# One attention block with a mixture of experts on one core: h and hn stored in two parts on other queues, the last ranks and slots earlier, and tile 2 in two passes

## The reference, cut to what matters

```python
def _layernorm(x, axis=-1, eps=1e-05):
    m = jnp.mean(x, axis=axis, keepdims=True)
    v = jnp.var(x, axis=axis, keepdims=True)
    return (x - m) / jnp.sqrt(v + eps)
...
    def _L0_xattn_ref(query, key):
        a = jnp.einsum('bqd,bkd->bqk', query, key)
        e = jax.nn.softmax(a, axis=-1)
        c = jnp.einsum('bqk,bkd->bqd', e, key)
        return c

    def _L0_ffn_ref(x, W_gate, b_gate, W_e, b_e):
        TOP_K = 2
        logits = x @ W_gate + b_gate
        _, top_idx = jax.lax.top_k(logits, TOP_K)
        y_all = jax.nn.relu(jnp.einsum('bsd,edh->bseh', x, W_e) + b_e)
        y = jnp.take_along_axis(y_all, top_idx[..., None], axis=2)
        return y.mean(axis=2)
    x = x + jnp.tanh(g_xattn[0]) * _L0_xattn_ref(_layernorm(x, axis=-1), ctx_4096)
    x = x + jnp.tanh(g_ffn[0]) * _L0_ffn_ref(_layernorm(x, axis=-1), L0_ffn_W_gate, L0_ffn_b_gate, L0_ffn_W_e, L0_ffn_b_e)
    return x
```

## Time and profile before

| | us |
|---|---|
| median of 3 runs | 343.68 (340.76 to 344.42) |
| the profiled execution | 344.42 |
| its span, first to last instruction | 342.5 |
| TensorE busy in the span | 319.5 (93%) |
| VectorE, ScalarE, GpSimd busy | 203.9, 122.9, 75.3 |
| mean granted TensorE clock | 0.98 |

### The profile page before, as it was taken

How to read it: one execution, slowest core, us unless ns; L and a number is a source line. 1 busy time by engine, 2 the same in 40 slices (tenths; PEclk the granted TensorE clock), 3 DMA queues, 4 the chain that set the end, 5 groups by cost and what they waited for, 6 DMA issues and landing times.

```text
span 342.5 us, 4328 instructions
## 1 busy us (share of the span) xinstructions
PE 319.5 (93%) x1510; PEld 235.1 (69%) x1510; DVE 203.9 (60%) x434; ACT 122.9 (36%) x165; POOL 75.3 (22%) x91
## 2 busy tenths in 40 slices
PE   5699999999999999959999999999999999999970
PEld 5344565565665588738788888888888888888850
DVE  2324457676668886886694975755176575753220
ACT  2223434625534558013345535515032551431000
POOL 6000110100103320303334321530120333011120
PEclk9969999999999999999999999999999999999995
DMA  7999999999948799567999999998359989634152
GB/s 253 303 288 303 349 353 332 354 319 362 389 156 292 268 382 327 147 225 206 379 340 367 353 355 354 255 381 273 61 169 346 282 215 382 208 61 63 10 84 31
DMA packets 24711, 90.57 MB, mean 264 GB/s; under 512 B 3276, under 2 KB 3276, under 8 KB 24680
## 3 DMA queue, kind: packets, MB, share of 16 engines
q1 hardware_dynamic: 13752, 52.86, 43.6%
q0 software_dynamic: 7792, 25.47, 28.5%
q10 hardware_dynamic: 3136, 11.83, 10.4%
HBM read 73.63 MB, written 16.52 MB: 263 GB/s over the span
## 4 chain that ended last, share of the span: by engine, by line
PE 80%; DMA 10%; DVE 4%; POOL 1%; ACT 1%; issue 1%; SPq 0%; DVEq 0%
PE ps L449 49%; PE ps L357 11%; PE ps L382 11%; DMA hn_rows<-hn 4%; PE ps L432 4%; DMA wg<-in_L_ffn_W_gate 3%; DMA xg<-hn_rows,src_token 2%; PE ps L403 2%; PE ps L394 1%; PE ps L348 1%; DVE stats L738 1%; DVE x_all L789 1%; DMA x_all<-in_x 1%; PE ps L365 1%; POOL guess L1117 1%
## 5 line engine op out<-in xcount | busy, mean ns | idle before, releaser
L449 PE MATMUL ps<-wh,xh 128*128 128x512 f32 x256 | 83.0, 400 | 0.1
L449 PE MATMUL ps<-wl,xh 128*128 128x512 f32 x256 | 80.4, 393 | 0.3 <-issue 0.3
L881 DVE TENSOR_TENSOR wl<-raw,wh 128x1024 fp32r<-128x1024 f32 x64 | 75.6, 1219 | 8.4 <-ACT wh L632 8.1
L449 PE MATMUL ps<-wh,xl 128*128 128x512 f32 x256 | 80.2, 393 | 0.0
L632 ACT ACTIVATE wh<-raw 128x1024 fp32r<-128x1024 f32 x64 | 63.7, 1051 | 22.9 <-DMA raw<-in_L_ffn_W_e 20.9
L449 PEld LDWEIGHTS ps<-wl,xh 128*128 128x128 f32 x256 | 48.0, 188 | 11.4 <-DVE wl L881 0.7
L449 PEld LDWEIGHTS ps<-wh,xl 128*128 128x128 f32 x256 | 48.0, 188 | 10.7
L449 PEld LDWEIGHTS ps<-wh,xh 128*128 128x128 f32 x256 | 46.4, 188 | 9.3 <-DVE xl L885 0.5
L1065 POOL DMA_INDIRECT out_rows<-y,dst_token x15 | 29.0, 1933 | 107.1 <-DVE y L895 88.5
L635 ACT ACTIVATE xh<-ps 128x1024 fp32r<-128x1024 f32 x16 | 16.4, 1024 | 90.1 <-PE ps L432 90.1
L357 PE MATMUL ps<-kT,qT 128*100 128x361 f32 x128 | 43.4, 493 | 1.0 <-ACT qT L611 1.0
(11 more groups left out here) (124 smaller groups left out, 240.0 us busy)
## 6 DMA issues: line engine op xcount, KB each, us to landing
raw<-in_L_ffn_W_e SPq DMA_DIRECT2D x64, 512.0 KB, 9.2
kT<-in_ctx_cols SPq DMA_DIRECT2D x16, 722.0 KB, 11.3
ctx<-in_ctx ACTq DMA_DIRECT2D x8, 1024.0 KB, 11.1
bias<-in_L_ffn_b_e SPq DMA_DIRECT2D x8, 512.0 KB, 10.9
ctx<-in_ctx ACTq DMA_DIRECT2D x8, 420.0 KB, 14.5
hn_rows<-hn POOLq DMA_DIRECT2D x8, 400.0 KB, 9.5
out_rows<-x_all POOLq DMA_DIRECT2D x2, 1600.0 KB, 19.1
x_all<-in_x SPq DMA_DIRECT2D x7, 384.0 KB
```

Of the source, the lines that this page charges most:

```text
L449: mm = nc.tensor.matmul(into[:, n * HB:(n + 1) * HB], rows[:, k, :], weights[:, k, n * HB:(n + 1) * HB], start=(k == 0 and c == first), st ...
L881: nc.vector.tensor_tensor(wl[e % 2][:, k, :], raw[e % 2][:, k, :], wh[e % 2][:, k, :], ALU.subtract).then_inc(s_wl, 1)
```

## The change

h goes out in two halves of four batches by `hidden`, each half as one DMA of rows 0 to 95 and one of rows 96 to 99 of each batch: the first half from ACT, behind the load of the last values, the second from SP, behind the weights of expert 1. The stores of zeros move from POOL to SP, behind that. hn is stored by POOL in the same two parts. In TensorE's stream, ranks of batch 7 move to chunk 0 and slots of batch 6 to chunk 1 of tile 0's last product, and slots of batch 7 and the second count to its chunk 6. DVE makes one low chunk of expert 1 before the token names instead of after. Tile 2 does HH and HL for all k, with tile 3's transposes behind chunk 5, and then LH; the low weights of expert 0 are handed back in the first pass, and a semaphore of its own (`s_wh0free`) hands back the high ones.

```diff
@@ -225,12 +225,13 @@
         s_slots = sem("slots_ready")
         s_tokens = sem("tokens_ready")
         s_table = sem("tile_table_ready")
-        s_hstore = sem("h_stored")
+        s_hstore = [sem(f"h_stored{h}") for h in range(HALVES)]
         s_hnstore = sem("hn_stored")
         s_zero = sem("spare_rows_zeroed")
         s_wh = sem("w_high_ready")
         s_wl = sem("w_low_ready")
         s_wfree = sem("w_used")
+        s_wh0free = sem("first_w_high_used")
         s_gath = [sem(f"gathered{t}") for t in range(2)]
         s_xT = sem("x_turned")
         s_xh = sem("x_high_ready")
@@ -262,7 +263,13 @@
                     eng.value_load(tile_table[0:1, 1, e:e + 1], min_val=0, max_val=OVER * E))
 
 
-        STORES = ((0, HALF_B), (HALF_B, B))
+
+        Q_SPREAD = Q // 16 * 16
+        X_PARTS = [(0, Q_SPREAD), (Q_SPREAD, Q)]
+
+        def hidden(half, first, end):
+            rows = out[half * HALF_TOK:(half + 1) * HALF_TOK, :].rearrange("(b q) d -> q b d", q=Q)
+            return rows[first:end], x_all[first:end, half * HALF_B:(half + 1) * HALF_B, :]
 
 
         FIRST_CHUNKS = {3: (0,), 4: (1,), 5: (2,), 6: (3,), 7: (4, 5), 8: (6, 7)}
@@ -284,10 +291,6 @@
 
         @block.sync
         def _(sp):
-
-            Q_SPREAD = Q // 16 * 16
-            X_PARTS = [(0, Q_SPREAD), (Q_SPREAD, Q)]
-
             def load_x(b):
                 for first, end in X_PARTS:
                     sp.dma_start(x_all[first:end, b, :], x[b, first:end, :]).then_inc(s_x[b - 1], 16)
@@ -325,8 +328,17 @@
             for k in range(KD):
                 load_weights(1, k)
 
+            sp.wait_ge(s_h, B)
+            for first, end in X_PARTS:
+                sp.dma_start(*hidden(1, first, end)).then_inc(s_hstore[1], 16)
+            sp.wait_ge(s_const, 1)
+            for t in range(HALVES):
+                rows = out[N_TOK + t * P:N_TOK + (t + 1) * P, :].rearrange("p (a d) -> p a d", d=256)
+                sp.dma_start(rows, zero[:, :].unsqueeze(1).to_broadcast([P, D // 256, 256])).then_inc(s_zero, 16)
+
             sp.wait_ge(s_hn, B)
-            sp.wait_ge(s_hstore, 16 * len(STORES))
+            for h in range(HALVES):
+                sp.wait_ge(s_hstore[h], 16 * len(X_PARTS))
             load_bias(0)
             load_bias(1)
             for e in range(2, E):
@@ -529,19 +541,19 @@
                     logits(B - 1)
             for k in range(KD):
                 mm = tile(0, k, (LH,), LH)
-                if k == 2:
+                if k == 0:
+                    ranks(B - 1)
+                if k == 1:
                     slots(B - 2)
-                if k == 4:
-                    ranks(B - 1)
+                if k == 6:
+                    slots(B - 1)
+                    counts(1)
             mm.then_inc(s_mm, 1)
 
             pe.wait_ge(s_xl, 2)
             for k in range(KD):
                 pe.wait_ge(s_wh, KD + k + 1)
                 tile(1, k, (HH, LH), None)
-                if k == 1:
-                    slots(B - 1)
-                    counts(1)
             for k in range(KD):
                 pe.wait_ge(s_wl, KD + k + 1)
                 mm = tile(1, k, (HL,), HL)
@@ -559,6 +571,14 @@
                     overflow(e, over, over_before)
                 if n + 1 < N_TILES and ORDER[n + 1][1] == 1:
                     over, over_before = overs(pe, ORDER[n + 1][0])
+                if n == 2:
+
+                    pe.wait_ge(s_xh, n + 1)
+                    for k in range(KD):
+
+                        tile(n, k, (HH, HL), None).then_inc(s_wfree, 1)
+                        if k == 5:
+                            turn_tile(n + 1)
                 pe.wait_ge(s_xl, n + 1)
                 if n == 3:
                     pe.wait_ge(s_yev, 1)
@@ -574,11 +594,11 @@
                 for k in range(KD):
                     if half == 0:
                         pe.wait_ge(s_wl, KD * e + k + 1)
-                    mm = tile(n, k)
+                    mm = tile(n, k, (LH,)) if n == 2 else tile(n, k)
                     if half == 1:
-                        mm.then_inc(s_wfree, 1)
+                        mm.then_inc(s_wh0free if n == 2 else s_wfree, 1)
                     if n + 1 < N_TILES:
-                        if k == 2:
+                        if k == 2 and n > 2:
                             turn_tile(n + 1)
                         if k == 5 and ORDER[n + 1][1] == 1:
                             first_over(ORDER[n + 1][0], over, over_before)
@@ -602,7 +622,7 @@
                 act.wait_ge(s_xn, b + 4)
                 if b > 0:
                     act.wait_ge(s_hT, 2 * b)
-                    act.wait_ge(s_hnstore, 16 * b)
+                    act.wait_ge(s_hnstore, 16 * len(X_PARTS) * b)
                 normalise(hn, b, 0, s_hn)
 
             def evacuate_turned(b, turned, banks, dst, done):
@@ -629,6 +649,8 @@
 
             def split_weights(e, k):
                 act.wait_ge(s_raw[e % 2][k], 16 * (e // 2 + 1))
+                if e == 2:
+                    act.wait_ge(s_wh0free, k + 1)
                 nc.scalar.activation(wh[e % 2][:, k, :], raw[e % 2][:, k, :], ACT.Copy).then_inc(s_wh, 1)
 
             def split_rows(high, turned):
@@ -645,7 +667,7 @@
                 if half == 0:
                     eng.wait_ge(s_mm, [t for t in ORDER if t[1] == 0].index((e, 0)) + 1)
                 else:
-                    eng.wait_ge(s_wfree, KD * (e + 1))
+                    eng.wait_ge(s_wh0free if e == 0 else s_wfree, KD if e == 0 else KD * (e + 1))
 
             def split_over(over_before, j):
                 act.wait_ge(o_xT, over_before + j + 1)
@@ -683,6 +705,11 @@
                 if 1 <= s and s + 1 < B:
                     act.wait_ge(s_att, s)
                     load_values(s + 1)
+                if s + 2 == B:
+
+                    act.wait_ge(s_h, HALF_B)
+                    for first, end in X_PARTS:
+                        act.dma_start(*hidden(0, first, end)).then_inc(s_hstore[0], 16)
             split_tile(0)
             normalise_hidden(B - 2)
             for k in FIRST_CHUNKS[B]:
@@ -900,7 +927,7 @@
                 if half == 0:
                     dve.wait_ge(s_mm, [t for t in ORDER if t[1] == 0].index((e, 0)) + 1)
                 else:
-                    dve.wait_ge(s_wfree, KD * (e + 1))
+                    dve.wait_ge(s_wh0free if e == 0 else s_wfree, KD if e == 0 else KD * (e + 1))
                 dve.wait_ge(s_bias[e % 2], 16 * (e // 2 + 1))
                 if n >= 2:
                     dve.wait_ge(s_added[n % 2], 16 * (n // 2))
@@ -951,14 +978,17 @@
             choose(B - 1)
             split_tile(1)
             locate(B - 1)
+
+            split_weights(1, 0)
             name_tokens(1)
-            for k in range(KD):
+            for k in range(1, KD):
                 split_weights(1, k)
                 if k == KD // 2:
                     fill_table()
             split_tile(2)
 
-            dve.wait_ge(s_hstore, 16 * len(STORES))
+            for h in range(HALVES):
+                dve.wait_ge(s_hstore[h], 16 * len(X_PARTS))
             dve.wait_ge(s_hn, B)
             dve.wait_ge(s_tgf, 1)
             evacuate(0)
@@ -1042,14 +1072,10 @@
             pool.wait_ge(s_const0, made[0])
             pool.nop().then_inc(s_const, 1)
 
-            def store_hidden(first, end):
-                pool.wait_ge(s_h, end)
-                rows = out[first * Q:end * Q, :].rearrange("(b q) d -> q b d", q=Q)
-                g.dma_start(rows, x_all[:, first:end, :]).then_inc(s_hstore, 16)
-
             def store_normed(b):
                 pool.wait_ge(s_hn, b + 1)
-                g.dma_start(hn_rows[b * Q:(b + 1) * Q, :], hn[:, :]).then_inc(s_hnstore, 16)
+                for first, end in X_PARTS:
+                    g.dma_start(hn_rows[b * Q + first:b * Q + end, :], hn[first:end, :]).then_inc(s_hnstore, 16)
 
             def gather(dst, idx, done, rows=hn_rows):
                 g.indirect_dma_start(dst[:, :], None, rows, bass.IndirectOffsetOnAxis(idx, 0)).then_inc(done, 16)
@@ -1125,20 +1151,12 @@
             for s in range(1, B + 1):
                 if s == HALF_B + 3:
                     pool.wait_ge(s_tokens, 1)
-                    pool.wait_ge(s_hnstore, 16 * HALF_B)
+                    pool.wait_ge(s_hnstore, 16 * len(X_PARTS) * HALF_B)
                     gather_tile(0)
                     gather_tile(1)
                 guess_root(s + 2, 0, 2 if s + 2 < B else 1)
                 store_normed(s - 1)
-                if s == B:
-                    store_hidden(*STORES[1])
-                if s + 1 == B:
-
-                    store_hidden(*STORES[0])
-                    for t in range(HALVES):
-                        rows = out[N_TOK + t * P:N_TOK + (t + 1) * P, :].rearrange("p (a d) -> p a d", d=256)
-                        g.dma_start(rows, zero[:, :].unsqueeze(1).to_broadcast([P, D // 256, 256])).then_inc(s_zero, 16)
-            pool.wait_ge(s_hnstore, 16 * B)
```

(6 more changed lines are left out.)

## The result

The changed kernel takes 345.74 us, median of 9 runs (342.93 to 346.63), beside 343.29 us for the kernel before (9 runs, 340.76 to 344.42). The ratio is 1.008, with a 95% interval of 1.0049 to 1.0111: 0.8% slower, above the range that was given. Of the rivals the second, with 345.4 us, came out. A time is the median of all runs of a kernel, while a ratio leaves out runs over 1.5% above its fastest, so the two can differ a little.

What follows compares the result with a forecast made beforehand. TensorE's 3.53 us hole at tile 2, behind the last hn store and the gather, was the bound. Gain 3.2 less costs 0.4, 0.3 and 0.1 gives 2.4 us: from 343.68 to 341.3 us, range 339.0 to 344.5.

Steps and rivals of the forecast that it cites:

- the second rival: Tile 0's gather takes the hole's place: all of h passes ahead, TensorE loses 4.9 us, 345.4 us; chance 0.09.
- the hole at tile 2: TensorE idles 3.53 us in 146 to 153, awaiting tile 2's gather; closing it was to gain 3.2 us.
- the 7.5 us for the last hn store: Batch 7's hn store, no longer behind h, was to take 7.5 us instead of 15.2, landing at 134.7.
- Cost (b): ACT's next normalisation waits for both parts of hn, which has one buffer: cost 0.3 us, bounds 0 and 1.8.
- Cost (c): Tile 4's gather, next to be late as expert 2's loads come closer together: cost 0.1 us, bounds 0 and 1.5.
- Two passes: Tile 2 in two passes has the same matmuls and TensorE doesn't wait for weights later: costed at nothing.
- cost (a): Tile 0's just-in-time gather slips 1.2 us behind h's early first half: cost 0.4 us, bounds 0 and 4.9.
- its sign of being wrong: A new wait over 1 us at tile 0's gather, its hn transposes or tile 4's transposes would refute the forecast.
- a fifth of free time: Argument against the rival on tile 0's gather: DMA engines are 0.80 busy in 107 to 111.
- The rule on the number of engines: A DMA uses the largest engine count up to 16 dividing its slowest dimension: 100 rows on 10, 96 on 16.

Runs made afterwards that it cites:

- experiment 1: The changed kernel with the first half of h stored by SP behind expert 1's weights instead of by ACT: 343.01 us, ratio 0.9966.
- experiment 3: The changed kernel with two batches of h (0.82 MB) in ACT's early store instead of four, six in SP's late one: 341.90 us, ratio 0.998.
- experiment 6: The changed kernel, expert 1's weights issued only after tile 0's gather landed: 345.37 us, ratio 1.0054; separately, tile 1's gather issued only then: 345.47 us, 1.0073.

## Why the prediction was wrong

**What held.** The bound was read rightly: the hole at tile 2 hung on the store of hn, and then on the names. The names ended at 139.78, 36.6 us behind the attention of batch 6, against 34.4 before: 2.2 us later, where the stream ahead of them was 4.3 us late, so 2.1 us were gained, 1.8 forecast. The hole gave back 3.8 us (4.3 late ahead of it, 0.5 behind it), 3.2 forecast. But that is not the gain alone, for TensorE came to the hole 4.3 us late. Where it doesn't come late, in experiment 1, the names end at 138.08, as forecast (138.25), but hn releases the gather 1.4 us behind them, and the hole gives back 2.1 us (tile 2's first product 45.22 us behind the attention of batch 6, against 47.33). So the 7.5 us for the last hn store were too few: its four rows took 9.5 us in the changed kernel (128.75 to 138.27) and 12.1 in experiment 3.

**Cost (b)**, the second part of hn, was put at 0.3 and measured nothing: no wait stands at batch 7's normalised rows, in the changed kernel or in experiment 1. **Cost (c)**, tile 4's gather, was put at 0.1 with bounds to 1.5 and measured 0.9: 12.26 us instead of 11.1, a wait of 1.00. **Two passes** at nothing held within what a run can tell.

**The step that failed is cost (a)**, tile 0's gather behind the first half of h: "I take 1.2 in all, since h is done before the gather is", and 0.4 after the idle time. Measured: a gather issued 0.5 us later and 3.4 us longer, a wait of 3.72 us, 4.3 us lost behind VectorE's choice. This is the new wait of over 1 us that the prediction named as its sign of being wrong. Its upper bound, 4.9, held it, and the second rival named the place and the cause; 0.09 was its chance. That the rival's 345.4 lies so near to 345.74 is in part luck: it has neither the clock nor tile 4 in it, and a gain of 3.2.

Three things were wrong in cost (a). First, its reason came true and didn't help: ScalarE's queue is done by 111.8 and the gather lands at 113.85, but in its first 4 us it hardly moves (0.05 MB on GpSimd's queue, 0.68 before), while 1.43 MB of ScalarE's pass. Second, its price is the difference of two stores of 0.4 MB, one beside a full queue and one in "a quiet stretch". That stretch was not quiet: in 103.93 to 109.67 the DMA share of before is 0.91. So 1.8 us says little of 1.64 MB in front. Third, a fifth of free time was named as an argument against, but not multiplied out: 2.2 us hold 0.79 MB, about half of h. That would have been a warning and not a price; the balance gives 2.4 of the 3.4 us and fails in experiment 6.

The Trainium skill, page "DMA: Bandwidth & Descriptors", section "Issuing engines are not separate DMA queues", which says that DMAs of all issuing engines share the same 16, was the right one of the two that were weighed: the gather's 11.04 us against 7.6 bear it out. The rule on the number of engines, weighed beside it, put (a) at its low end; its 10 of 16 engines would also be a share of 0.63 in the tail, which shows 0.37.

The second error is the clock. The prediction looked at it for the hole that goes (1.00 there) and not for the wait that might come. That wait cost 1.4 us more than its length in the profile, and filling it took 1.0% off the ratio.

**What stays open**: why the gather needs 7.0 us behind its first 4, also with engines free, how the clock's cost lies between 1.4 and 3.4 us, when the clock falls at tile 0, and the 351 us of the early store in the kernel before.

## What to carry to other kernels

Before a transfer is moved ahead of a gather that is just in time, multiply the idle share of the DMA engines over that gather's stretch by its length. Here that gave 2.2 us, 0.79 MB; a store of 0.82 MB went free and one of 1.64 MB didn't. Two sizes in one kernel make no law, and what a larger store costs was not given by its bytes, so try a store of about that size first, rather than a half. A wait moved to another place may cost more there than where it was, so read the clock at the new place too. And a hole that closes behind a new loss may have closed because of it: compare the gain with a kernel that lacks the loss.

## What the runs showed of the hardware

- A wait of TensorE of 3.2 us at tile 2 left the granted clock at 1.00. Waits of 2.7 to 4.4 us at tile 0 came with means of 0.57 to 0.79 in 112 to 120, and eight transposes at 1.34 to 1.97 us instead of 1.07; so did one of 0.51 us (0.79, 1.69 us), while two of 0.26 and 0.16 us left it at 1.00. Directly ahead of tile 0 stand the small matmuls of the logits and three transposes, ahead of tile 2 full matmuls of tile 1. With 1.73 us of transposes ahead of it a wait of 1.67 us left the clock at 1.00.
- On the same engines 0.82 MB of h on ScalarE's queue cost a gather of GpSimd's nothing (7.60 us), and 1.64 MB cost it 3.4 us. In the first 4 us after its issue GpSimd's queue moved 0.68 MB with no h, 0.36 with half of it and 0.05 with all.
- A gather can be late with engines free: 11.02 us at a DMA share of 0.84, against 11.04 at 0.98 with weights beside it.
- Two executions reach the same step 2.5 us apart (24.63 and 27.14), ahead of the first edited store; kernels are better compared from a common step than by their spans.
